# A one-core transformer-like block on Trainium2: the attention part's input matrices in three passes of split operands, and the first layer's engine orders rearranged

## The reference, cut to what matters

```python
def _L0_ffn_ref(x, norm_w, w1, w3, w2, gate_w, a1, b1, a3, b3, a2, b2):     # block A
    nx = x * rsqrt(mean(x * x) + EPS) * norm_w;  t = nx
    topw, topi = top_k(softmax(t @ gate_w.T), 2)          # weights of 2 of 8 experts
    h1 = (t @ w1.T)[None] + 2.0 * (t @ a1[e].T) @ b1[e].T
    h3 = (t @ w3.T)[None] + 2.0 * (t @ a3[e].T) @ b3[e].T
    act = silu(h1) * h3
    out_e = act @ w2.T + 2.0 * (act @ a2[e].T) @ b2[e].T
    return sum over the 2 chosen experts of weight * out_e
def _L0_attn_ref(x, ...):                                  # the attention part
    h = layernorm(x)
    v = h @ Wv + bv;  f, i = sigmoid(h @ Wf), sigmoid(h @ Wi);  o = sigmoid(h @ Wo + bo)
    attn = causal sum of v weighted by i and the products of f, divided by the weights' sum
    x = x + o * attn
    m = layernorm2(x) @ W1 + b1                            # W1 is 128 x 384
    return x + square(leaky(m)) @ W2 + b2                  # the "middle block"
```

## Time and profile before

| | |
|---|---|
| time, median of 3 runs | 1070.97 us (1069.66 to 1073.24) |
| the profiled execution | 1072.74 us, of it span 1071.0 us |
| busy PE / DVE / ACT / POOL | 983.1 / 704.7 / 505.9 / 496.8 us |
| granted TensorE clock, mean | 0.989 of full |
| first layer | from 0 to about 697 us of the span |

### The profile page before, as it was taken

The page is one execution under the profiler, slowest core; times in us unless marked ns, Lnnn a source line. Parts: engine busy times, 40 slices in busy tenths (PEclk is TensorE's granted clock), DMA queues, the critical chain, the costliest instruction groups (busy, mean ns, idle before and its releaser), DMA issues. The chain is left out here.

```text
span 1071.0 us, 15568 instructions
## 1 busy us (share of the span) xinstructions
PE 983.1 (92%) x4422; PEld 670.3 (63%) x4429; DVE 704.7 (66%) x2142; ACT 505.9 (47%) x1039; POOL 496.8 (46%) x483
## 2 busy tenths in 40 slices
PE   2999999999999999998999999989997999989994
PEld 1766666556575655655666667458773667648873
DVE  4787878786786868767968886535452567644552
ACT  2433444555556565553544433234452777614542
POOL 2446454544545445443536545524443144443444
PEclk9999999999999999998999999999999999999998
DMA  6069000000000000000000000236544000015651
GB/s 178 1 252 419 19 0 1 1 1 1 1 1 1 1 1 1 1 0 2 1 11 11 3 8 11 82 90 187 177 154 140 2 14 19 21 52 162 185 176 47
DMA packets 42900, 65.12 MB, mean 61 GB/s; under 512 B 7153, under 2 KB 25121, under 8 KB 40640
## 3 DMA queue, kind: packets, MB, share of 16 engines
q1 hardware_dynamic: 37824, 55.59, 15.9%
q0 software_dynamic: 4992, 8.54, 2.4%
HBM read 37.20 MB, written 28.74 MB: 62 GB/s over the span
## 5 line engine op out<-in xcount | busy, mean ns | idle before, releaser
L358 PE MATMUL bank<-split 128*128 128x512 f32 x416 | 206.9, 497 | 16.8 <-ACT wT L898 8.4
L360 PE MATMUL bank<-split 128*128 128x512 f32 x416 | 165.3, 397 | 0.0
L359 PE MATMUL bank<-split 128*128 128x512 f32 x416 | 164.7, 396 | 0.0
L859 ACT ACTIVATE sil<-bank 128x512 f32<-128x512 f32 x128 | 76.6, 599 | 115.4 <-PE bank L360 109.9
L1620 POOL TENSOR_TENSOR gsum<-act 128x512 f32<-128x512 f32 x64 | 84.9, 1327 | 90.5 <-DVE act L1193 90.5
L412 PE MATMUL bank<-act,a 128*128 128x512 f32 x256 | 118.9, 598 | 0.0
L358 PEld LDWEIGHTS bank<-split 128*128 128x128 f32 x416 | 79.2, 191 | 59.9 <-issue 21.2
L1189 DVE TENSOR_TENSOR act<-bank,sil 128x512 f32<-128x512 f32 x128 | 87.7, 685 | 21.4 <-PE bank L360 19.1
L359 PEld LDWEIGHTS bank<-split 128*128 128x128 f32 x416 | 79.7, 192 | 29.1 <-issue 18.8
L684 PE MATMUL bank<-xlT,e 128*128 128x256 f32 x368 | 88.7, 384 | 6.6 <-issue 3.9
L1193 DVE TENSOR_TENSOR act<-act,wT 128x512 f32<-128x512 f32 x128 | 89.9, 702 | 4.4
(11 more groups left out here) (282 smaller groups left out, 1951.3 us busy)
## 6 DMA issues: line engine op xcount, KB each, us to landing
e<-e_dram SPq DMA_DIRECT2D x92, 256.0 KB, 3.1
rows_in<-yw SPq DMA_DIRECT2D x17, 1056.0 KB, 17.8
xin<-rows_in SPq DMA_DIRECT2D x46, 132.0 KB, 3.0
x<-rows_out SPq DMA_DIRECT2D x8, 256.0 KB, 4.7
rows_in<-yw,slot_i POOLq DMA_INDIRECT x64, 2.3
rows_out<-ob,ids POOLq DMA_INDIRECT x46, 2.3
out<-ob,ids POOLq DMA_INDIRECT x46, 2.4
act<-b_dram SPq DMA_DIRECT2D x2, 256.0 KB, 3.3
```

The lines of the kernel that those rows point to most:

```text
L358: mm(dst, w[0], m[0], start=start, stop=False, **more)
L359: mm(dst, w[0], m[1], start=False, stop=False, **more)
L360: return mm(dst, w[1], m[0], start=False, stop=stop, **more)
L859: af(sil[(k - 1) % 2][:, :], bank[BH1[STEPS[k - 1][0] % 2]][:, :], ACT.Silu).then_inc(silu_done.sem, 1)
```

## The change

The four gate and value matrices (`wif` spread to two squares, `wo`, `wv`) and the middle block's `wm1` are split once, in slot 3 (ACT copies, `gates_low` on DVE), and applied with `mm3` to split activations. The activation parts live in `hT_split`, which shares its place with `iv`, `r2`, `num` and `den`. ACT gets a copy (`a_high`, `a_mid_high`), POOL a subtraction (`a_low`, `a_mid_low`) for each, both from SBUF. `mask(3)` is made from `mask(2)`'s copy in SBUF, and `up(0)` waits for three mask copies instead of four. `r_T` uses bank `BV`. For the first chunk `up(0)` and `up(1)` run ahead of the masks in banks of their own, and the splitting of block A's weights is divided between DVE and POOL. Several steps stand elsewhere in the four lists.

```diff
-        wm1 = sb("wm1", [P, JM * P]); bm1 = sb("bm1", [P, JM]); wm2 = sb("wm2", [P, JM, P])
+        gates_w = sb("gates_w", [P, 8 * P], F32R); wm1_w = sb("wm1_w", [P, 2 * JM * P], F32R)
+        gate_w = [tuple(gates_w[:, (2 * i + k) * P:(2 * i + k + 1) * P] for k in range(2)) for i in range(4)]
...
+        with nc.sbuf_tensor("hT_split", [P, 4 * S], F32R) as hT_split:
+            hTs, h2Ts = (tuple(hT_split[:, (2 * i + k) * S:(2 * i + k + 1) * S] for k in range(2)) for i in range(2))
+        iv, r2, num, den = (sb(n, [P, S]) for n in ("iv", "r2", "num", "den"))
...
+        GATES = [(d, w) for d, w in zip(gate_w, [wif[:, k:k + 1].to_broadcast([P, P]) for k in range(2)] + [wo, wv])] + [(wm1s, wm1)]
+        LOW_DVE, LOW_POOL = (0, 1, 3, 5), (2, 4)
...
+                    if g == 0 and e == 0:
+                        pe.wait_ge(weight_rest.sem, i + 1)
+                        pe.wait_ge(weight_low.sem, i + 3)
...
-                    if i == 0:
-                        pe.wait_ge(*maskT_saved(q))
+                    if q == 0:
                         pe.wait_ge(*t_low(q))
-                        if q == 0:
-                            pe.wait_ge(weight_low.sem, 6)
+                        pe.wait_ge(weight_low.sem, i + 1)
+                    elif i == 0:
+                        pe.wait_ge(*maskT_saved(q, 3))
+                        pe.wait_ge(*t_low(q))
                     else:
                         pe.wait_ge(*u_masked(q, 2))
-                    mm3(bank[BPRE][:, :], (a1s, a3s)[i], ts[q % 2], True, True).then_inc(u_ready.sem, 1)
+                    mm3(u_bank(q, i)[:, :], (a1s, a3s)[i], ts[q % 2], True, True).then_inc(u_ready.sem, 1)
...
-                    if s.a_norm is not None:
-                        pe.wait_ge(*z_ready(s.a_norm))
-                    if s.r_sort is not None:
-                        pe.wait_ge(*top1_steps(s.r_sort, 1))
-                    if s.a_down is not None:
-                        pe.wait_ge(*xa_done(s.a_down))
-                    if s.a_up is not None:
-                        pe.wait_ge(*h2T_saved(s.a_up))
-                    transpose4(BSIDE, lambda t: yn4[n % 4][:, t, :]).then_inc(ynT_r.sem, 1)
+                    pe.wait_ge(*r_done(MAINS - 1 if l is None else l))
+                    transpose4(BV, lambda t: yn4[n % 4][:, t, :]).then_inc(ynT_r.sem, 1)
...
-                    pe.wait_ge(*h2T_saved(n))
-                    if j == 0 and s.r_pre is not None:
-                        pe.wait_ge(*xnT_saved(s.r_pre))
+                    pe.wait_ge(*h2T_low(n))
+                    if n == 0 and j == 0:
+                        pe.wait_ge(gate_low.sem, 5)
                     if j:
                         pe.wait_ge(*m_saved(n, j))
-                    mm(bank[BSIDE][:, :], wm1[:, rows(j)], h2T[:, :], start=True, stop=True).then_inc(m_ready.sem, 1)
+                    mm3(bank[BSIDE][:, :], tuple(w[:, rows(j)] for w in wm1s), h2Ts, True, True).then_inc(m_ready.sem, 1)
...
-                    pe.wait_ge(*hT_saved(n))
+                    pe.wait_ge(*hT_low(n))
...
-                h(1, 3); h(3, 3)
+                h(1, 3)
                 fill(2)
                 r_aff()
+                h(3, 3)
                 logits()
+                if q == 0:
+                    up(0); up(1)
                 a_out()
...
                 h(1, 6)
-                a_mid(0)
                 h(3, 6)
                 mask(0)
                 down(0)
-                a_mid(1)
+                a_mid(0)
                 h(1, 7)
                 mask(1)
                 h(3, 7)
-                a_mid(2)
+                a_mid(1)
                 down(1)
                 mask(2)
+                h(1, 8)
+                a_mid(2)
+                if q != 0:
+                    up(0)
+                h(3, 8)
                 fill(4)
                 r_rank()
-                h(1, 8)
-                up(0)
-                h(3, 8)
                 value(0, (0, 1))
                 a_gate(0)
-                up(1)
+                if q != 0:
+                    up(1)
                 value(0, (2, 3))
                 a_gate(1)
                 down(2)
...
-                    act.wait_ge(*maskT_ready(q, min(n + 1, 3)))
+                    if n < 3:
+                        act.wait_ge(*maskT_ready(q, n + 1))
+                    else:
+                        act.wait_ge(*maskT_saved(q, 3))
...
-                        ins = af(dst[:, :], bank[BPRE][:, :], ACT.Copy, scale=-1.0, bias=1.0)
+                        ins = af(dst[:, :], wT[q % 2][0][:, :], ACT.Copy, scale=-1.0, bias=1.0)
...
-                        for k, w in enumerate((wi_b, wf_b)):
-                            af(w[:, :], wif[:, k:k + 1].to_broadcast([P, P]), ACT.Copy).then_inc(spread.sem, 1)
+                        for dst, w in GATES:
+                            af(dst[0], w, ACT.Copy).then_inc(gate_high.sem, 1)
...
+                def a_high():
+                    n = s.a_gate
+                    if n is None:
+                        return
+                    act.wait_ge(*hT_saved(n))
+                    act.wait_ge(*scan_steps(n - 1))
+                    af(hTs[0], hT[:, :], ACT.Copy).then_inc(hT_high.sem, 1)
+
+                def a_mid_high():
+                    n = s.a_up
+                    if n is None:
+                        return
+                    act.wait_ge(*h2T_saved(n))
+                    act.wait_ge(*oa_ready(n + 1 if s.a_norm is not None else n))
+                    af(h2Ts[0], h2T[:, :], ACT.Copy).then_inc(h2T_high.sem, 1)
...
                 pre_T()
+                a_high()
                 a_mid_norm()
                 silu(3)
                 a_norm(0)
+                if s.a_gate is not None:
+                    r_norm(s.r_pre)
                 a_out()
...
-                r_T(s.r_pre, BSIDE)
+                r_T(s.r_pre, BV)
+                a_mid_high()
                 silu(6)
+                mask(0)
                 a_mid(0)
-                mask(0)
-                a_mid(1)
                 silu(7)
                 mask(1)
-                a_square(0)
-                a_mid(2)
+                a_mid(1)
                 mask(2)
                 mask(3)
+                a_square(0)
+                silu(8)
+                a_mid(2)
+                up_high(0)
                 a_square(1)
-                silu(8)
-                up_high(0)
                 a_square(2)
                 a_gates()
                 up_high(1)
                 a_norm(1)
-                r_norm(s.r_stat)
+                if s.a_pre is None:
+                    r_norm(s.r_stat)
...
+                    for n in some:
+                        dst, w, f = SPLITS[n]
                         dve.wait_ge(weight_high.sem, n + 1)
                         v.scalar_tensor_tensor(dst[1], w, f, dst[0].bitcast(F32), ALU.mult, ALU.subtract).then_inc(weight_low.sem, 1)
...
+                    for n, (dst, w) in enumerate(GATES):
+                        dve.wait_ge(gate_high.sem, n + 1)
+                        v.scalar_tensor_tensor(dst[1], w, 1.0, dst[0].bitcast(F32), ALU.mult, ALU.subtract).then_inc(gate_low.sem, 1)
+
...
                 second_values()
+                r_read(s.r_sort, BSIDE)
                 a_mid_stats()
                 act(3)
-                r_top1(s.r_sort, BSIDE)
+                r_top1(s.r_sort)
+                split_low(LOW_DVE[:2])
...
                 top2(1)
+                split_low(LOW_DVE[2:])
...
                 f_stats()
-                split_low()
                 act(6)
...
                 a_leaky(1)
-                r_rows(s.r_sort, BSIDE)
+                gates_low()
                 masked(0)
                 act(8)
                 a_leaky(2)
                 masked(1)
+                r_rows(s.r_sort, BSIDE)
...
+                    if q == 0:
+                        for n in LOW_POOL:
+                            dst, w, _ = SPLITS[n]
+                            pool.wait_ge(weight_high.sem, n + 1)
+                            pool.tensor_tensor(out=dst[1], in0=w, in1=dst[0].bitcast(F32), op=ALU.subtract).then_inc(weight_rest.sem, 1)
...
+                    pool.wait_ge(*hT_high(n))
+                    if l is not None:
+                        pool.wait_ge(*r_ready(l))
+                    pool.tensor_tensor(out=hTs[1], in0=hT[:, :], in1=hTs[0].bitcast(F32), op=ALU.subtract).then_inc(hT_low.sem, 1)
...
+                    pool.wait_ge(*h2T_high(n))
+                    pool.tensor_tensor(out=h2Ts[1], in0=h2T[:, :], in1=h2Ts[0].bitcast(F32), op=ALU.subtract).then_inc(h2T_low.sem, 1)
...
                 total(0)
                 a_mid_scale()
+                a_low()
                 total(1)
+                a_mid_low()
                 f_scale()
+                mask_diff()
                 a_scale()
                 r_scale(s.r_stat)
-                mask_diff()
                 total(2)
                 total(3)
...
```

(5 more changed lines are left out.)

88 lines of the change are left out of this document (51 added, 37 removed).

## The result

| kernel | time, us | ratio to before, 95% interval |
|---|---|---|
| before | 1071.84 (1069.66 to 1073.24) | 1 |
| changed | 1058.94 (1054.89 to 1059.74) | 0.9874 [0.9843, 0.9905] |

The account below looks back on a forecast made before the run. TensorE's own work was taken as the bound, with 21.5 us of waits between, and a DVE-ACT chain almost equally long in slots 5 to 10. Gains by slot summed to 20.4, from 1072.74 to 1052.3, said as 1052; range 1042 to 1065.

Parts of the forecast that it names:

- rival (a): Slots 5 to 10: TensorE's clock falls ahead of the gates, 1.7 us each, 10 in all, giving 1062; chance 0.28.
- the waits that go: TensorE would no longer wait for `wT` ahead of `up(0)`, nor for `lg` or `hT`.
- the wait for `gi`: In slots 5 to 10 TensorE's second gate would wait 1 to 2 us for `gi`.
- the stretched products: DVE's `act * wT` products would take 1.2 to 1.7 us about POOL's `a_low` and `a_mid_low`.
- the start of `h(1,2)`: In the first chunk `h(1,2)` could start at 30.2, 3.4 us earlier; 2.7 taken as gain.
- reserve of 1.68: DVE's idle time ahead of `ua` in slot 8, 1.68 us, against which its added delays were set.
- the interval of 1.5 to 2.7: How much later DVE would be ahead of `ua`, from `a_high`'s delay and POOL's locks: 1.5 to 2.7 us.
- for slots 6 to 9 I take 0.1 us each: Slots 6 to 9: shorter gates and DVE's delay nearly cancel, a gain of 0.4 us together.
- five splits on DVE eat part of it: Slot 3: gain of 0.7 us, from 0.4 and 0.7 of the gates, less part for DVE's weight splits.
- The term for slot 11: Slot 11: waits for `lg`, lost clock and `r_T`'s bank give 6.7 less the locks, 5.0 us taken.
- The 9.5 us: TensorE time saved by three passes for four: 8 chunks x 7 products x 0.17 us.
- rival (b): Slots 4 to 11: POOL's locks on DVE do not meet, 8 us more gained, 1044; chance 0.20.

Follow-up runs that it names:

- high_late: The changed kernel with ACT's `a_high` moved behind `a_mid_norm`: 1053.52 us, ratio 0.9833.
- low_early: The changed kernel with POOL's `a_low` moved ahead of `total(0)`: 1058.91 us, ratio 0.9871.
- both_moved: The changed kernel with `a_low` ahead of `total(0)` and `a_high` behind `a_mid_norm`: 1052.98 us, ratio 0.9826.
- free_passes: The changed kernel, three passes kept, rounded activation written at once and used as low part too, no activation copies or subtractions: 1047.44 us, ratio 0.9782.
- hidden_parts: The changed kernel with `a_high` ahead of `pre_T` and `a_low` on DVE ahead of `a_mix`, where those engines wait: 1047.36 us, ratio 0.9777.
- splits_early: The changed kernel with DVE's five weight splits of slot 3 moved behind `act(2)`, from ahead of `masked(0)`: 1054.80 us, ratio 0.9849.
- best: The changed kernel with the moves of `hidden_parts` and `splits_early`, and `a_mid_stats` ahead of `second_values`: 1041.47 us, ratio 0.9730.
- mdiff_late: The changed kernel with POOL's `mask_diff` back behind the two powers (`a_scale`, `r_scale`): 1075.25 us, ratio 1.0042.
- orders_alone: The changed kernel with gates, values and `wm1` back as plain float32 products, without their copies, low parts and splits; orders as changed: 1043.52 us, ratio 0.9743.
- stats_first: `orders_alone` with DVE's `a_mid_stats` moved ahead of `second_values`: 1042.67 us, ratio 0.9744.
- passes_alone: The kernel before, in its own orders, with only the three-pass products, their copies, subtractions and weight splits: 1090.42 us, ratio 1.0207.

## Why the prediction came out as it did

**The number.** The median, 1058.94, is 7 above the forecast of 1052 and only 3 below rival (a)'s 1062. That it is no further off is in part luck: the sum misses by 2.5 us, but its terms by up to 3 each, with both signs, and the other 4 us lie behind the first layer. Of the signs that the prediction named, the waits that go, the wait for `gi`, the stretched products and the start of `h(1,2)` came true, and so did one that was to show it wrong, the clock of rival (a).

**Right, and shown.** The waits of TensorE that were to go are gone, and with the passes left away the orders are worth 27 us. How much of that is the bank waits' was not run apart; the move of `mask_diff` is among these orders. Start: `h(1,2)` was forecast at 30.2 and ran at 30.34, behind the wait of 3.34 for the first low part; the start up to slot 2 gave 5.80 for 5.3. Slot 4 gave 1.52 for 1.6, slot 10 3.11 for 3.6, the stretch from slot 13 on 1.45 for 1.5. `a_high` ahead of `a_mid_norm` costs its 0.5 us a slot (`high_late`: 45.59 to 45.09). Two locks of 0.97 each and 0.52 against a reserve of 1.68 are inside the interval of 1.5 to 2.7. The Trainium skill (SBUF — State Buffer, section Who interferes with whom) has a DVE instruction with two SBUF inputs contend with a GpSimd instruction that reads SBUF, and lists `tensor_scalar` among those that can, when its operands meet the conditions of a 2-port mode. The trace agrees for the product, which took 0.97 longer, and the 128x4 `sc_z`, a `tensor_scalar`, took 1.06 longer; whether it meets those conditions no run shows.

**Mis-sized: "for slots 6 to 9 I take 0.1 us each".** They lost 2.55 together. At full clock a slot is 45.6, up to 0.3 longer than before and not 0.1 shorter, which is about 0.8 for the four. The rest is the clock: two falls of 1.35 lie in these lines (7 and 9), where before one of about 1.0 lay (46.38 in line 6). The third fall is in line 10. That is rival (a), at less than half its strength. "Lost each time at 1.7" became three times in six at 1.35. The wait was 2.0 us in all five of slots 5 to 9. Nine kernels with the gates in the changed order have such waits (the change, `low_early`, `high_late`, `both_moved`, `free_passes`, `hidden_parts`, `splits_early`, `best`, `mdiff_late`): 34 of 1.65 to 2.01 us ahead of the second gate in slots 5 to 10, 15 of them with a mean clock of 0.96 up to the next `ua`. Of the 32 waits of up to 1.32 us there, in these kernels, `orders_alone` and `stats_first`, none has one. So such a wait was nearly a coin toss, and the forecast should have charged it half a fall. The Trainium skill (TensorE: Matmul & The Clock Gate, section What's actually happening) has the gate's check run free of the kernel's own timing; equal waits with and without a fall agree with that.

**Mis-sized: slots 3 and 5.** Slot 3 was to give 0.7 since "five splits on DVE eat part of it". They ate all of it: `splits_early` gets 2.4 us back by moving them. Slot 5 was to give 1.0 and lost 0.68; without parts and passes it gives 1.51, and so it does in `free_passes`, so the copies and subtractions cost 2.2 there, in the first slot with both of them. The timeline of TensorE has 1.6 of that as waits; in `free_passes` the first is 0.18 and the second is not there, and `hidden_parts` still has the second:

```profile
222.21 1.12 PE L437 MATMUL bank<-gsum,w 128*128 128x512 f32 x2 [0.99 <-DVE x L1321]
223.94 0.50 PE L368 MATMUL bank<-hT_split,wm_w 128*128 128x512 f32 x1 [0.61 <-POOL hT_split L1760]
```

**Mis-sized: slots 11 and 12.** 7.68 came for 5.0 and 2.63 for 1.3. The term for slot 11 was "6.7 less the locks". Next to nothing was to be subtracted: the gates end with slot 10, so `a_low` does not run in slot 11. One product is locked there (1.58 us at 483.62), but TensorE, busy 43.99 of 46.28 us, has no wait for DVE behind it. The windows give a mean clock of 0.94 before and 1.00 after, 3.2 of 53.96 us, which is near the 3.4 taken. In slot 12 no product is locked.

**Missed: what `mask_diff` is worth.** The prediction counted the waits for `ud` that it takes away in slots 1, 2 and 4, 2.8 us, and in slots 5 to 9 charged its new place with "up to 0.25". It did not say what would follow there if the move were left away: DVE's reserve is gone, `ua` comes at once, and `mdT` would be late by 1.4 us a slot. The forecast holds in spite of this, since only the move as made entered its sum.

**Missed: what the passes are worth.** The 9.5 us were called "the most that it can give, and only where TensorE, not the chain, ends last", and that is right as a bound. The sum then took next to nothing for slots 6 to 9, gain and cost together. The passes with their parts are a loss of 12.4 us up to the first tile as built (15 by the medians) and a gain of about 2.4 when nothing has to be made for them. The cost is mostly in places, not in the work: `hidden_parts` has the same operations and gets 11.6 back. The rival (b), locks that do not meet, was put at 1044. `hidden_parts`, at 1047.4, is near to that case: no product is locked in the lines of slots 6 to 9, but `a_high`'s half microsecond is gone too, which (b) had kept.

**The last 4 us.** The code behind the first layer is the same in all kernels, and from the first `xin` to the end it took 363.3 us before, 367.3 in the changed kernel, and 364.1 to 368.8 in the experiments. In the changed kernel TensorE waits 5.2 us for `xin` and 2.5 for `x<-rows_out`, where it waited 2.3 and 0.5 before; `low_early` waits 6.7 and 1.6, `orders_alone` 5.0 and 0.4 in that part. The length goes roughly with TensorE's idle time there, all waits together: 27.8 us before, 30.5 in the changed kernel, 32.6 in `low_early`, 27.4 in `best`. It does not follow the two DMA waits alone: `passes_alone` has 6.5 us of them and takes 365.7, `hidden_parts` 4.7 and takes 366.4. Each kernel has one profile, and the cause stays open; the phase in which the first layer ends is one that no run tests. Of the profiled execution's miss, 1058.82 against 1052.3, it is 4.0 of 6.5 us.

## What to carry to other kernels

When an edit adds an operation to one engine and takes time from another, look for the idle time of the engines that can do it, ahead of a wait that is there in any case, and put it there: the same parts cost 12 us up to the first tile in one place and 2 in the other. Judge the two halves of a change apart before timing the whole, since a good order hides a bad split. Where a list has just lost its reserve, walk through all that feeds it, since what was slack there a moment ago is now worth its full length in every slot.
